# Slot attention with new slots and squares on GpSimd, squares summed by TensorE, and new orders on VectorE and TensorE

## What is computed

```
Pn = rmsnorm(P, input_norm_w); k_proj = Pn @ Wk.T; v_proj = Pn @ Wv.T     # P: 16 x 1500 x 128
for _ in range(3):
    sn = slots * rsqrt(mean(slots * slots, -1) + EPS) * slot_norm_w
    scores = (sn @ Wq.T) @ k_proj.T * SCALE
    attn = softmax(scores, over the slots)
    attn = attn / (sum(attn, over the keys) + EPS)
    updates = attn @ v_proj
    r, z, n = the gates of a GRU cell of (updates, slots)
    slots = (1 - z) * n + z * slots
x = x + tanh(g_xattn[1]) * slots
```

## Time and profile before

| what | value |
|---|---|
| median of 3 runs | 568.03 us (567.38 to 568.72) |
| the profiled execution | 568.96 us, its span 567.2 us |
| slot attention | about 239 to 452 us of the span |
| busy over the span | PE 479.8 us, DVE 358.0, ACT 321.6, POOL 210.8 |
| instructions | PE 6484, DVE 1029, ACT 959, POOL 366 |

### The profile page before, as it was taken

The page is one execution under the profiler, slowest core; times in us unless marked ns, Lnnn a source line. Parts: engine busy times, 40 slices in busy tenths (PEclk is TensorE's granted clock), DMA queues, the critical chain, the costliest instruction groups (busy, mean ns, idle before and its releaser), DMA issues.

```text
span 567.2 us, 17702 instructions
## 1 busy us (share of the span) xinstructions
PE 479.8 (85%) x6484; PEld 364.5 (64%) x6484; DVE 358.0 (63%) x1029; ACT 321.6 (57%) x959; POOL 210.8 (37%) x366
## 2 busy tenths in 40 slices
PE   4894988999796999879999998999998588489980
PEld 2531225566573454458999987899997458479980
DVE  0789964677627354458889888788888544023333
ACT  2564763555411122379999999899999240033330
POOL 8293862222420000034555445445544203602331
PEclk9996996999797799999999999999999988879996
DMA  8762643444149970600000498000000596120013
GB/s 333 251 222 97 209 165 101 136 138 141 48 160 418 356 93 1 259 40 2 4 3 17 185 365 319 4 4 3 0 0 3 200 426 283 50 78 21 26 31 106
DMA packets 30566, 75.17 MB, mean 133 GB/s; under 512 B 6669, under 2 KB 22078, under 8 KB 29486
## 3 DMA queue, kind: packets, MB, share of 16 engines
q1 hardware_dynamic: 26062, 62.47, 32.1%
q0 software_dynamic: 1424, 7.81, 3.7%
q10 hardware_dynamic: 3024, 4.13, 2.2%
HBM read 69.85 MB, written 4.54 MB: 131 GB/s over the span
## 4 chain that ended last, share of the span: by engine, by line
PE 39%; ACT 20%; DVE 18%; issue 8%; POOL 7%; DMA 5%; ACTq 1%; POOLq 1%; DVEq 0%; SPq 0%
ACT work L864 14%; PE ps L1561 5%; PE ps L1762 4%; PE ps L1469 4%; PE ps L1776 3%; PE ps L1595 3%; DVE ps L1200 2%; POOL xe_scratch L751 2%; PE ps L1423 2%; POOL rq L696 2%; PE ps L1616 2%; PE ps L1541 2%; DMA region<-in_ctx_blk 2%; PE ps L1644 2%; ACT work L881 2%
## 5 line engine op out<-in xcount | busy, mean ns | idle before, releaser
L864 ACT ACTIVATE work<-ps,nb,rkey 125x56 f32<-125x56 f32 x576 | 179.6, 514 | 4.6 <-DVE nb L1208 4.4
L1630 PEld LDWEIGHTS ps<-work,region 128*61 128x61 f32 (+1 forms) x2304 | 75.2, 136 | 8.2 <-issue 5.0
L1630 PE MATMUL ps<-work,region 128*61 128x56 f32 (+1 forms) x2304 | 76.3, 221 | 4.1 <-ACT work L864 3.7
L1644 PE MATMUL ps<-region,work 125*64 125x129 f32 x1152 | 73.5, 274 | 3.2 <-POOL work L715 1.9
L715 POOL TENSOR_TENSOR work<-work,rs 125x336 f32<-125x336 f32 x96 | 70.6, 756 | 3.8
L1644 PEld LDWEIGHTS ps<-region,work 125*64 125x64 f32 x1152 | 64.8, 136 | 4.6 <-POOL work L715 2.6
L1217 DVE TENSOR_REDUCE sm<-work 125x6 f32<-125x336 f32 x96 | 45.5, 492 | 17.5 <-ACT work L864 17.5
L1200 DVE TENSOR_REDUCE ps<-ps 125x6 f32<-125x336 f32 x96 | 44.4, 504 | 0.8 <-PE ps L1630 0.7
L1616 PE MATMUL ps<-GI,work 112*64 112x112 f32 (+3 forms) x288 | 34.7, 309 | 5.8 <-DVE work L1264 3.1
L708 POOL TENSOR_TENSOR rs<-rs,rkey 125x12 f32<-125x12 f32 x48 | 10.3, 215 | 75.7 <-DVE rs L1226 75.7
L1469 PE MATMUL ps<-xln,folded 128*128 128x448 f32 x64 | 29.9, 592 | 10.0 <-ACT region L791 10.0
(11 more groups left out here) (303 smaller groups left out, 999.2 us busy)
## 6 DMA issues: line engine op xcount, KB each, us to landing
region<-in_ctx_wide SPq DMA_DIRECT2D x16, 774.0 KB, 7.0
early_w<-in_ctx SPq DMA_DIRECT2D x16, 768.0 KB, 4.3
region<-in_w SPq DMA_DIRECT2D x6, 2048.0 KB, 19.8
region<-in_ctxT SPq DMA_DIRECT2D x16, 750.0 KB, 9.2
work<-in_ctxT_blk SPq DMA_DIRECT2D x22, 187.5 KB
early_w<-in_w POOLq DMA_DIRECT2D x1, 4096.0 KB, 12.4
region<-in_ctx_blk ACTq DMA_DIRECT2D x11, 192.0 KB, 2.8
early_w<-in_ctx_blk ACTq DMA_DIRECT2D x10, 192.0 KB, 2.5
```

The costliest lines, as they stand in the source:

```text
L864: i = act.activation(shares_of(p, a, h)[:, c, :], ps[:CP, 2 + 2 * h + a, c * S:(c + 1) * S], ACT.Exp, bias=nb[:, a, q:q + 1], scale=rkey[: ...
L1630: mm = pe.matmul(ps[r0:r1, 2 + 2 * h + a, c * S:(c + 1) * S], keysT[:, s, c0 + r0:c0 + r1], qT[:, p, a * S:(a + 1) * S], start=True, stop= ...
L1644: mm = pe.matmul(ps[i * COL:(i + 1) * COL, bank, 0:KW], A[:CP, p % 2, i, h, c * S:c * S + COL], keys[:, 2 * p + i, h * CH + c, :], start=( ...
```

## The change

- ACT's Square with sum is gone. POOL squares the slots elementwise (`slot_squares`), PE multiplies the squares with a column of ones (which sums them over the 128 features and puts the sums on the slots' partitions), and DVE adds epsilon on the way out of PSUM (`slot_sums`). POOL keeps the power.
- PE's `slot_proj` has 128 moving columns in place of 256, and then one column for the squares.
- The new slots, `finish` and `first_slots` go from DVE to POOL, which does them at the start of its phase, before `weights`; DVE keeps `finish` for the last two cells and the first two copies. ACT's tanh of the gates now waits until POOL has read the older z and n.
- The order on DVE and PE is new.

```diff
+            def slot_squares(x, p):
+                if not isinstance(x, int) or x >= 2:
+                    gp.wait_ge(q_proj, x - 1)
+                gp.wait_ge(sl_ok, x + 1)
+                gp.tensor_tensor(slot_sq[:, p % 2, 0:QS], slots_x[:, p, :], slots_x[:, p, :], ALU.mult).then_inc(q_ss, 1)
+            def slots_new(v_, p, dst):
+                gp.wait_ge(gru_n, v_ + 1)
+                gp.tensor_tensor(dn, slots_x[:, p, :], nt, ALU.subtract).then_inc(gru_new, 1)
+                gp.tensor_scalar(zt, zt, 0.5, 0.5, ALU.mult, ALU.add).then_inc(gru_new, 1)
+                gp.wait_ge(gru_new, v_ * 3 + 2)
+                gp.tensor_tensor(dn, zt, dn, ALU.mult).then_inc(gru_new, 1)
+                gp.wait_ge(gru_new, v_ * 3 + 3)
+                return gp.tensor_tensor(dst, dn, nt, ALU.add)
+            def finish(v_, g, p):
...
+                slots_new(v_, p, dn).then_inc(gru_last, 1)
+                gp.wait_ge(gru_last, 2 * n + 1)
+                gp.tensor_tensor(dn, dn, gates[:, 1:2].to_broadcast([128, QS]), ALU.mult).then_inc(gru_last, 1)
+                gp.wait_ge(gru_last, 2 * n + 2)
+                gp.tensor_tensor(xT[:, pair(g, p)], dn, xT[:, pair(g, p)], ALU.add).then_inc(x_new, 1)
...
-            def gates_of(v):
-
+            def gates_of(v, old_slots):
+                if old_slots:
+                    act.wait_ge(*old_slots)
                 act.wait_ge(gate_mm, v + 1)
...
-            def slot_sums(x, a):
-                act.wait_ge(q_proj, x + 1)
-                act.activation(slot_sq[:QS, a, :], ps[:QS, 7 - a, 128:256], ACT.Square, accum_out=ss[:, a:a + 1]).then_inc(q_ss, 1)
...
+            def slot_sums(x, a):
+                v.wait_ge(q_proj, x + 1)
+                v.tensor_tensor(ss[:, a:a + 1], ps[:QS, 7 - a, 128:129], eps_sum[:, :], ALU.add).then_inc(q_eps, 1)
...
-                by_columns(ps[:, bank, 0:256], slots_x[:, p, :], GI[:, :, :].rearrange("p a d -> p (a d)")).then_inc(q_proj, 1)
+                by_columns(ps[:, bank, 0:128], slots_x[:, p, :], GI[:, 0, :], skip_group_check=True)
+                pe.wait_ge(q_ss, x + 1)
+                by_columns(ps[:, bank, 128:129], slot_sq[:, p % 2, 0:QS], ones[:, 0:1], skip_group_check=True).then_inc(q_proj, 1)
...
                 scores_ahead(6)
-                scores_ahead(7)
                 if cell_runs(g, c):
                     gru_gates(v_ - 1)
-                update(g, c % TWO, v_, 0, 6 + c % 2)
+                scores_ahead(7)
                 if renews(g, c):
                     queries(v_ + 2, 6 + (c + 1) % 2)
+                update(g, c % TWO, v_, 0, 6 + c % 2)
                 update(g, c % TWO, v_, 1, 6 + c % 2)
```

More of the change, by code:

```diff
@@ L257, in build_program @@
         qT = qT_all.rearrange("p (a s) -> p a s", a=TWO)
-        Un, rt, zt, nt, tmp = (carve(QS, "work") for _ in range(5))
+        Un, rt, zt, nt, tmp, dn = (carve(QS, "work") for _ in range(6))
         Pn = carve(128, "work")
@@ L691, in slot_rms @@
             def slot_rms(x, a):
-                gp.wait_ge(q_ss, x + 1)
-                gp.tensor_tensor(ss[:, a:a + 1], ss[:, a:a + 1], eps_sum[:, :], ALU.add).then_inc(q_eps, 1)
                 gp.wait_ge(q_eps, x + 1)
@@ L715, in weigh, with first_slots @@
                 gp.tensor_tensor(shares_of(p, a, h), shares_of(p, a, h), bcast(rs[:, a, c], S), ALU.mult).then_inc(a_att, 1)
+            def slot_squares(x, p):
[12 more added lines that the diff above has]
+            def finish(v_, g, p):
+                n = g * TWO + p
+                gp.wait_ge(x_new, 4 + n)
+                slots_new(v_, p, dn).then_inc(gru_last, 1)
[3 more added lines that the diff above has]
+                gp.tensor_tensor(xT[:, pair(g, p)], dn, xT[:, pair(g, p)], ALU.add).then_inc(x_new, 1)
+            def first_slots(g, p):
+                gp.tensor_copy(slots_x[:, p, :], xln[:, pair(g, p)]).then_inc(sl_ok, 1)
+            for x in range(2):
+                slot_squares(x, x)
             for x in range(2):
@@ L721, in phase @@
                 p = c % TWO
+                old = (c - 2) % TWO
+                if cell_ends(g, c):
+                    if leaves(c):
+                        finish(v_ - 2, g - (c < 2), old)
+                    else:
+                        slots_new(v_ - 2, old, slots_x[:, old, :]).then_inc(sl_ok, 1)
+                if leaves(c) and renews(g, c):
+                    first_slots(g + (c >= 2), old)
+                if renews(g, c):
+                    slot_squares(v_ + 2, old)
                 weights(g, p, v_, 0)
@@ L877, in candidate_of @@
                 act.activation(nt, tmp, ACT.Tanh, bias=bih[:, 2:3]).then_inc(gru_n, 1)
-            def slot_sums(x, a):
-                act.wait_ge(q_proj, x + 1)
-                act.activation(slot_sq[:QS, a, :], ps[:QS, 7 - a, 128:256], ACT.Square, accum_out=ss[:, a:a + 1]).then_inc(q_ss, 1)
             act.wait_ge(a_pad, 1)
-            for x in range(2):
-                slot_sums(x, x)
             for m in range(LOOK):
@@ L1274, in _ @@
             for x in range(2):
-                first_slots(0, x)
+                v.tensor_copy(slots_x[:, x, :], xln[:, pair(0, x)]).then_inc(sl_ok, 1)
             v.wait_ge(q_pad, 1)
             v.wait_ge(a_pad, 1)
+            for x in range(2):
+                slot_sums(x, x)
             for x in range(2):
@@ L1287, in phase @@
             def phase(g, c, v_):
-                old = (c - 2) % TWO
                 p = c % TWO
@@ L1311, in phase @@
                     update(v_ - 1, 6 + (c + 1) % 2)
+                maxima_ahead(4)
                 reciprocals(p, v_, 0)
-                if cell_ends(g, c):
-                    if leaves(c):
-                        finish(v_ - 2, g - (c < 2), old)
-                    else:
-                        gru_slots_new(v_ - 2, old, slots_x[:, old, :]).then_inc(sl_ok, 1)
-                if leaves(c) and renews(g, c):
-                    first_slots(g + (c >= 2), old)
-                maxima_ahead(4)
                 maxima_ahead(5)
+                negated_ahead(4)
+                sums_ahead(2)
                 if cell_runs(g, c):
                     gru_inputs(v_ - 1)
-                negated_ahead(4)
-                sums_ahead(2)
+                if renews(g, c):
+                    slot_sums(v_ + 2, c % 2)
                 sums_ahead(3)
@@ L1331, in phase @@
                 maxima_ahead(7)
-                sums_ahead(4)
                 if cell_runs(g, c):
```

18 lines of the change are left out of this document (9 added, 9 removed).

## The result

The changed kernel takes 564.23 us (median of 20 runs, 561.82 to 568.40), the kernel before 569.66 us (20 runs, 567.38 to 571.33). The ratio is 0.9914, 95% interval 0.9895 to 0.9933: faster by 4.9 us (3.8 to 6.0); the two medians stand 5.4 us apart. The forecast was 6.4 us.

A forecast was written before the change was run, and what follows sets the result against it. PE and ACT were both taken as nearly full; gains of 3.7 (steady cells), 1.6 (change of groups), 0.7 (end) and 0.4 (start) sum to 6.4 us, taking the 568.03 us median to 561.6, range 557.5 to 566.0.

The forecast's parts named there:

- PE becomes the one bound: Steady cell: PE's 7.76 us exceeds ACT's 7.56, so the cell falls from 7.98 to 7.76 us.
- One sign: Steady cell: ACT would show idle times for the first time, 0.2 us per cell.
- The projection at 0.36 us: PE's slot projection with one-column matmuls takes 0.36 us (0.35 to 0.66) in place of 0.47, saving 0.11 per cell.
- rival A: PE keeps its 7.97 us per cell because narrow matmuls cost what the halving saves, or a wait opens; 565.3 us, 16%.
- The wait of 0.10 us on PE: PE's second 48 score matmuls wait 0.10 us per cell for ACT's exponentials; the change removes all of it.
- price: Each of POOL's new 128x112 instructions takes 0.40 us.
- The doubt about 0.2 us per cell at the second weighing: POOL finishes the second weighing at 6.6 us against 6.4 needed; uncovered, 0.2 us per cell eats the whole gain.
- rivals C and D: C: POOL's chain sets the pace, 579 us, 5%. D: POOL's lateness eats the steady gain, 567 us, 6%.
- Change of groups: Four cells there take 8.3 us each in place of 8.7, PE waiting for POOL's squares; 1.6 us gained.
- End: Last phases: ACT's 0.74 us wait for DVE's negated maxima goes, POOL is about 0.25 us late; 0.7 us gained.
- Start: First normalization, waiting 2.51 us, comes sooner as POOL squares beside PE's projection; 0.4 us gained.
- the second look at the earlier trace: A DVE new-slot instruction took 0.78 us, not 0.27, with 0.51 of waiting on POOL's SBUF reads; adds nothing to the sum.

The follow-up runs named there:

- p1_wide: Changed kernel with 256 moving columns in the slot projection again, the upper 128 unused; 569.14 us, steady cell 8.03 us.
- a1_act_load: Changed kernel with an added, unread 128x128 Square on ACT in each cell; 563.36 us, steady cell 7.81 us.
- p2_no_bias: Changed kernel without the four one-row PE matmuls per cell that add the candidate's hidden bias; 564.65 us.
- b1_no_square: Kernel before without ACT's Square (sums of squares left out, power of a constant), with an early one-column exponential; 568.97 us, cell 7.92 us.
- g1_pool_one: Changed kernel with one added 128x112 multiplication per cell on POOL behind the squares; 562.03 us.
- t3_late_finish: Changed kernel with an early exponential, without two filler matmuls, and with POOL's gate and addition to x at phase end at group changes; 562.26 us.
- after_again: The changed kernel run again unchanged; 563.14 us, ratio 0.9885 to the kernel before.
- g2: Changed kernel with three added 128x112 multiplications per cell on POOL behind the squares; 574.01 us.

## Why the forecast held, and where it did not

- **PE becomes the one bound: right**, and shown by p1_wide (0.22 us added on PE, 0.22 on the cell) and a1_act_load (0.20 added on ACT, nothing on the cell); p2_no_bias shows that the next limits are only 0.1 to 0.3 us away. The counts are as forecast (PE 6580, DVE 975, ACT 911, POOL 472). One sign did not come: ACT shows no idle time in the steady cell. Its slack is there, but hidden under the records.
- **The projection at 0.36 us: right** (0.34), and so was the choice near the lower bound; rival A needed 0.47.
- **The wait of 0.10 us on PE: half as large.** b1_no_square gives back 0.05. The forecast took all of the difference between the two 48 scores (1.44 - 1.34) for wait, so that 96 would take 2.68 us; in the changed kernel they take 2.74, of 2.78 before. The cell came to 7.81 in place of 7.76, and the 17 steady cells to 2.8 us in place of 3.7.
- **POOL: right as to price** (0.42, 0.29 and 0.37 us for the forms, 0.40 forecast) and as to the steady cells. The doubt about 0.2 us per cell at the second weighing, and rivals C and D with it, fell: POOL idles 1.4 us there, and only three added instructions make the cell longer. The Trainium skill (GPSIMD Engine Reference, Engine selection) has GpSimd at about twice VectorE's time for two inputs. The forecast held 0.40 against the 0.27 of another operation. The subtraction that moved takes 0.42 us on POOL (L725) and 0.21 on DVE before, as this row of DVE's timeline shows, so the trace agrees: twice. In the steady cell it costs nothing, as PE's work covers it.

```profile
322.21 0.21 DVE L1250 TENSOR_TENSOR work<-work 128x112 f32<-128x112 f32 x1
```

- **Change of groups: right in size, wrong in place.** 1.6 forecast, 1.8 to 2.1 measured. PE waits for the queries, because the power stands behind POOL's longer chain, and not before the projection for the squares.
- **End: 0.7 forecast, 1.5 measured.** The wait of the earlier trace rows went as told. In the last two cells more goes than that. PE waited 0.95 us for the gates of the last cell but one, as the first row shows (timeline of PE, before), and waits 0.44 now (the second).

```profile
441.24 0.80 PE L1616 MATMUL ps<-work,F1w 128*64 128x112 f32 x12 [0.95 <-DVE work L1239]
```

```profile
438.82 0.80 PE L1650 MATMUL ps<-work,F1w 128*64 128x112 f32 x12 [0.44 <-DVE work L1275]
```

- **Start: the failed step.** "I take 0.4" for the sums on POOL and PE; it lost 1.36. The chain itself did get shorter: with the table out of the way it is 6.75 for 6.98, 0.2 us. But the Square that went was also the work behind which ACT's table load could run without a wait. I counted the instructions that the change removes, and not what stood in the shade of them. With 1.6 us for that, the forecast would have been 563.2.
- **The total came out better than its terms, and that is luck.** The steady cells were forecast 0.9 us too high and the start 1.8, the end 0.8 too low and the change of groups 0.2 to 0.5; so 6.4 stands beside 4.9 to 5.15. The forecast median of 561.6 lies 2.6 us under the measured 564.23, and 1.6 of these come from the kernel before, whose 20 runs have a median of 569.66 where the three at hand had 568.03.

Two rows of the changed kernel's last cells, where DVE still makes the new slots, bear on the second look at the earlier trace rows:

```profile
441.46 0.58 DVE L1287 TENSOR_TENSOR work<-work 128x112 f32<-128x112 f32 x1 [0.52 <-ACT work L920]
...
448.78 0.28 DVE L1287 TENSOR_TENSOR work<-work 128x112 f32<-128x112 f32 x1 [0.45 <-ACT work L920]
```

```profile
440.46 1.46 POOL L713 TENSOR_TENSOR work<-work,rs 125x336 f32<-125x336 f32 x2
```

The same instruction takes 0.58 us beside POOL's weighing, until 442.04, when that is over (441.92), and 0.28 when POOL is idle. This is what the Trainium skill (SBUF — State Buffer, Who interferes with whom) states, and in the slot attention of the changed kernel it is seen only here.

## What to carry to other kernels

When an instruction is removed, ask what its engine did behind it without a wait: a table load may then fall behind the next wait, and a one-column activation of the same function ahead of that wait gives it back (1.6 us here). Where two engines are nearly full, add a little work to each in turn: the one that passes it on to the period, one for one, is the bound, whatever the busy shares say. Work moved to a slack engine cost nothing in the steady cell here, but at the change of groups, where that engine has most to do, an instruction ahead of the one that others wait for counts for most of its length (0.24 to 0.30 of 0.35 us in g1_pool_one); move behind it what can wait (1.36 us in t3_late_finish).

## What the runs showed of the hardware

- An ACT_TABLE_LOAD takes 1.28 us. The one ahead of the first exponential, which waits, started only when that wait was over (0.39 us after the negated maxima were ready).
- TensorE's clock fell behind a wait that another engine caused. In all eight profiles in which the table load is late, PE waits 3.05 us for the first exponentials, and the granted clock falls to 0.50 for some microseconds, during this wait or shortly behind it. In the profiles with the early load and the filler, and in the kernel before, this wait is 1.40 to 1.46 us, and the clock stays at 1.00. Windows of after_again (PE's busy time second, the clock third from the end):

```profile
247.00:249.00 2.00, 0.00 (x0) 0.00 (x0) 0.49 (x2) 1.99 (x6) 0.00 (x0) 0.96 0.01 4
249.00:254.00 5.00, 3.96 (x67) 3.84 (x69) 2.42 (x7) 5.00 (x19) 1.36 (x3) 0.50 0.00 0
```

  It costs nothing here: from the first exponential to `UnN` of the first cell the changed kernel and its versions, all but g2, take 11.7 us, with the fall or without. ACT shows no idle time in this stretch, so it sets the pace there.
- The code ahead of the stage is the same in all kernels, and reached it at 237.1 to 242.2 us of the span. Why is open.
- The stall marked "issue" on PE at the change of groups (0.66 to 1.48 us, in three profiles with a second one of 0.37 to 0.66) stood in all profiles but three (after_again, g1_pool_one, g2_pool_three), and once was there and once not in the same kernel. What it is was not settled.
